# Thirteen loads of the next attention head, issued by ScalarE instead of SyncE

## The reference, cut to what matters

```
Q, K, V = proj(q_w), proj(k_w), proj(v_w)          # per head: two halves of 32, values of 64
attn1 = softmax(Q1 @ K1.T * scale)
attn2 = softmax(Q2 @ K2.T * scale)
out = (attn1 - lam * attn2) @ V                     # then an RMS norm over the head, an output projection
```

## Time and profile before

| | us |
|---|---|
| median of 3 runs | 6037.92 (6028.88 to 6040.64) |
| profiled execution | 6063.87 |
| its span on the core | 6062.1 |
| first and last `take_out` of the stage | 311.6 and 3228.1 |

### The profile page before, as it was taken

The page is one execution under the profiler, slowest core; times in us unless marked ns, Lnnn a source line. Parts: engine busy times, 40 slices in busy tenths (PEclk is TensorE's granted clock), DMA queues, the critical chain, the costliest instruction groups (busy, mean ns, idle before and its releaser), DMA issues. The chain is left out here.

```text
span 6062.1 us, 84099 instructions
## 1 busy us (share of the span) xinstructions
PE 5460.9 (90%) x23692; PEld 3112.7 (51%) x23692; DVE 3506.3 (58%) x4330; ACT 2393.7 (39%) x5287; POOL 3071.3 (51%) x1607
## 2 busy tenths in 40 slices
PE   8799999999999999999996979999997988897970
PEld 4455555555555555555553434554554555554540
DVE  3477777777777777777774543443443444443228
ACT  3255555555555555555552211322322333332430
POOL 0198888988888988888883102544441000000001
PEclk9799999999999999999997886999998999998995
DMA  6601111101111011111013643112201000000121
GB/s 224 190 16 40 41 42 42 37 19 42 42 42 42 18 39 40 42 41 41 15 41 94 179 147 73 37 37 53 58 16 61 21 21 21 21 10 30 47 92 69
DMA packets 244613, 330.97 MB, mean 55 GB/s; under 512 B 87260, under 2 KB 224754, under 8 KB 234490
## 3 DMA queue, kind: packets, MB, share of 16 engines
q1 hardware_dynamic: 244218, 326.08, 19.4%
HBM read 202.49 MB, written 123.51 MB: 54 GB/s over the span
## 5 line engine op out<-in xcount | busy, mean ns | idle before, releaser
L654 POOL TENSOR_TENSOR diff_run_pool<-diff_run_pool,diff_probs 128x768 f32<-128x768 f32 x1152 | 2235.1, 1940 | 187.8 <-ACT diff_probs L502 100.6
L582 DVE TENSOR_REDUCE diff_maxes<-diff_max 128x1 f32<-128x768 f32 x1752 | 1571.7, 950 | 676.3 <-PE diff_max L404 675.5
L502 ACT ACTIVATE diff_probs<-diff_ring 128x384 f32<-128x384 f32 x3462 | 1398.8, 495 | 956.9 <-PE diff_ring L394 843.0
L430 PE MATMUL diff_out_ps<-diff_probs,diff_vs 128*64 128x384 f32 x6912 | 1272.5, 504 | 0.0
L394 PE MATMUL diff_ring<-diff_qs,diff_ks 97*128 97x384 f32 x3462 | 1076.5, 385 | 19.6 <-issue 10.1
L404 PE MATMUL diff_max<-diff_ks,diff_qs 96*128 96x384 f32 x3504 | 953.9, 354 | 98.8 <-DVE diff_maxes L582 65.0
L394 PEld LDWEIGHTS diff_ring<-diff_qs,diff_ks 97*128 97x128 f32 x3462 | 607.3, 188 | 552.1 <-issue 360.1
L430 PEld LDWEIGHTS diff_out_ps<-diff_probs,diff_vs 128*64 128x64 f32 x6912 | 453.0, 139 | 559.3 <-issue 360.5
L404 PEld LDWEIGHTS diff_max<-diff_ks,diff_qs 96*128 96x128 f32 x3504 | 613.0, 193 | 148.3 <-DVE diff_maxes L582 95.5
L2083 POOL MEMSET pick_before<- 128x128 f32 x1 | 0.2, 204 | 1311.0 <-POOLq L63 1311.0
L1299 DVE TENSOR_REDUCE causal_maxes<-causal_max 128x1 f32<-128x384 f32 x522 | 288.7, 554 | 522.2 <-PE causal_max L1180 316.4
(11 more groups left out here) (228 smaller groups left out, 5935.9 us busy)
## 6 DMA issues: line engine op xcount, KB each, us to landing
diff_qs<-qk_hi SPq DMA_DIRECT2D x68, 288.0 KB, 7.7
diff_ks<-qk_hi SPq DMA_DIRECT2D x68, 288.0 KB, 10.1
diff_recip<-row_factors SPq DMA_DIRECT2D x194, 96.0 KB, 2.7
o_rows<-diff_normed SPq DMA_DIRECT2D x97, 192.0 KB, 1.8
qk_hi<-proj_hi SPq DMA_DIRECT2D x12, 1536.0 KB, 5.8
qk_lo<-proj_lo SPq DMA_DIRECT2D x12, 1536.0 KB, 9.6
causal_qa<-qk_hi SPq DMA_DIRECT2D x120, 96.0 KB, 2.5
diff_qs<-qk_lo SPq DMA_DIRECT2D x34, 288.0 KB, 8.8
```

Source lines behind the costliest of these rows:

```text
L430: mm = pe.matmul(out_ps[VD * j:VD * (j + 1), 0:T], vs[par][:, g, j, :], probs[g % PBUF][:, j * T:(j + 1) * T], start=g == 0, stop=g == STE ...
L502: act.activation(probs[g % PBUF][:, j * T:(j + 1) * T], ring[bank][:, 0:T], ACT.Exp, scale=SCALE).then_inc(s_taken, 1)
L582: dve.tensor_reduce(maxes[side][:, row:row + 1, h], max_ps[u % 2][:, :, 0:T], AX.XY, ALU.max).then_inc(s_red, 1)
L654: pool.tensor_tensor(run_pool[:], acc[:], probs[g % PBUF][:], ALU.add).then_inc(s_accp, 1)
```

## The change

ACT issues the 13 loads instead of SP. It does so in slot 0 of a head's first chunk, behind the six exponentials that it handles in that slot. SP no longer waits for the last product of values, and keeps the sums' trip and the stores. Since the loads' addresses are written out as constants, ACT's loop over 8 pairs of heads becomes straight code; PE, DVE and POOL keep their loops. The first head's loads stay on SP. In the kernel before, the second head's loads are issued ahead of chunk 0's work, behind the first head's; in the changed kernel they fall into chunk 0.

```diff
+        def load(eng, par, b, h):
+            for j in range(2):
+                for dst, kind, parts in ((qs, 0, (qh, qh, ql)), (ks, 1, (qh, ql, qh))):
+                    for r, src in enumerate(parts):
+                        eng.dma_start(dst[par][j][r * HD:(r + 1) * HD, :].bitcast(F32),
+                                      src[b * 2 * H0 + kind * H0 + h, j, :, :]).then_inc(s_ld[par], 16)
+            eng.dma_start(vs[par][:, :, 0, :], v_tiles[:, b * NT:(b + 1) * NT, h, :]).then_inc(s_ld[par], 16)
...
-                load(0)
+                load(sp, 0, 0, 0)
...
                 for q in range(CHUNKS):
-                    if q % NC == 0:
-
-                        sp.wait_ge(s_pv, q * BATCHES + BATCH)
-                        load(q // NC + 1)
                     invert_sums(q - 1)
                     store(q - 1)
...
-                with act.Fori(0, HEADS // 2) as i:
+                for i in range(HEADS // 2):
                     for m in range(2 * NC):
                         q, m1 = i * (2 * NC) + m, (m + 1) % (2 * NC)
                         for slot in range(BATCHES):
...
                                 exps(q + 1, 0)
+                            if slot == 0 and m % NC == 0:
+                                nxt = (q // NC + 1) % HEADS
+                                load(act, nxt % 2, nxt // H0, nxt % H0)
                             if slot == ROWS_AT:
```

More of the change, by code:

```diff
@@ L322, in differential_attention @@
             "normed_ready", "stored"))
+        qh = qk_hi.rearrange("b (h j d) n -> (b h) j d n", j=2, d=HD)
+        ql = qk_lo.rearrange("b (h j d) n -> (b h) j d n", j=2, d=HD)
+        v_tiles = v_rows.rearrange("(t p) (h d) -> p t h d", p=P, d=VD)
+        def load(eng, par, b, h):
[5 more added lines that the diff above has]
+            eng.dma_start(vs[par][:, :, 0, :], v_tiles[:, b * NT:(b + 1) * NT, h, :]).then_inc(s_ld[par], 16)
         with nc.Block() as block:
@@ L329, in _ @@
                 sp.dma_start(ident_sb[:], ident).then_inc(s_const, 16)
[L331 to L343, removed]
                 def invert_sums(q):
```

## The result

The changed kernel took 6162.67 us (median of 4 runs, 6136.54 to 6171.92) beside 6039.28 (4 runs) for the kernel before: a ratio of 1.0197, interval 1.0157 to 1.0236. Run again later (experiment 5), the ratio was 1.0107, 1.0076 to 1.0138, with a median of 6137.49 against 6064.34 for the kernel before. It is slower, as forecast, by 1 to 2%. The two intervals belong to one and the same pair of kernels and do not overlap, so a ratio here is good to about 1%, and smaller effects are read from the traces. Both medians lie above the range given (5998 to 6120).

What follows compares the result with a forecast made beforehand. PE is busy 90% of the span; row sums waiting behind loads at head starts were taken to cost 121.6 us. Terms 20 + 31.5 + 11.1 gave +62.6 on the median 6037.9: 6100 us, range 5998 to 6120.

Steps and rivals of the forecast that it cites:

- the sum over the first chunks: Attention stage, first chunks of heads: 20 us inside the body, 31.5 behind the branch, 11.1 in chunk 0, together +62.6 us.
- the first term: Eight head starts inside the loop's body: each 2.5 us slower than now, 20 us in all.
- the second: Seven head starts behind the branch: each 4.5 us slower than now, 31.5 us in all.
- the third: Chunk 0: 5.6 us for ACT's part and 5.5 for the wait that is left, 11.1 us.
- Part one: ACT's 13 issues take 6.1 us; exponentials come 3.6 us late, clock adds 2: a first chunk's first half 5.6 late.
- the price of the clock: PE's granted clock falls behind its stop for ACT's issues: put at 2 us per head start.
- Part two: Loads begin later: 2.5 us inside the body, 4.5 behind the branch, where only 1.1 of ACT's issue time is exposed.
- part four: ACT's loop as straight code: saves ACT's branch, 0.7 us at seven places; idle time hides the rest, costed at nothing.
- Part three: SP free of loads: row sums still held in SP's issue until loads are nearly through; compact sums at 483.4, not 480.90.
- the first rival: At head starts, SP's row sums pass ACT's loads: -23 us, about 6014; chance 0.33.
- its sign, a short issue: SP's issue of the row sums taking well under 5 us, or half a us, would show the sums passing the loads.
- The range: Whole kernel's time: 5998 to 6120 us, leaving out the cases near 5925 and 6180.

Runs made afterwards that it cites:

- experiment 5: The changed kernel run once more with more rounds, against the kernel before: ratio 1.0107, median 6137.49 us against 6064.34.
- experiment 3: The changed kernel with all 13 loads issued by ACT in slot 3 instead of slot 0, behind the row sums' trip: 6101.4 us, ratio 1.0058.
- experiment 1: The kernel before with only ACT's loop written out as straight code, loads still on SP: ratio 1.0049 to the kernel before.
- experiment 2: The changed kernel with 12 of ACT's loads in slot 0 and the values' load in slot 3: 6085.7 us, ratio 1.0023.
- experiment 6: The kernel before with straight code on ACT, loads on SP, and the wait for PE's bank given first: ratio 1.0023.
- experiment 8: The changed kernel with ACT's issues spread, two per slot from slot 3, and the wait for PE's bank given first: ratio 0.9835.

## Why the prediction was right or wrong

**Right: the side, and the sum over the first chunks.** From the starts of `take_out`: the eight first chunks inside the body grew from 37.99 to 40.27 in the mean, 18.2 us in all (forecast 20); the seven behind the branch from 36.98 to 42.30, 37.2 us (31.5); chunk 0 ended 7.4 us later (11.1). Together 62.8, against 62.6. That the two sums meet so closely is luck: the first term was 1.8 too high, the second 5.7 too low, the third 3.7 too high (the 480.8 in its working stands in no row).

**Part one** held: 13 issues in 6.1 us, a stop of PE of 3.3 us, the clock behind it. Only the price of the clock was low: experiment 3 has 6.6 us for such a stop alone, where I took 5.6. In the second head of the changed kernel the row sums are issued 16.9 us behind `take_out` instead of 10.5, 6.4 later; over the eight heads inside the body it is 15.6 in the mean, 5.1 later, where I had 5.6.

**Part two** held inside the body: the first load is issued 2.2 us behind `take_out` (2.5). Behind the branch it was issued 4.0 us behind it, but my claim that ACT's stop would be mostly covered there failed. With ACT's own branch gone, the clock did not fall in slot 0 (1.00 from 655 to 666 us, where it was 0.52 from 647 to 654 before), so PE ran into the full stop:

```profile
656.31 0.62 PE L388 MATMUL diff_ring<-diff_qs,diff_ks 97*128 97x384 f32 x2 [1.62 <-issue]
...
658.80 0.32 ACTq L332 DMA_DIRECT2D diff_qs<-qk_hi  x1
...
665.56 0.44 PE L388 MATMUL diff_ring<-diff_qs,diff_ks 97*128 97x384 f32 x1 [3.42 <-ACT diff_probs L496]
```

That is a stop of 3.42 us where I had 1.1. It lies ahead of the wait for the row sums, which becomes shorter by it, and is not what made the branch term 5.7 us short. By experiment 1 the shortfall belongs to part four: with straight code alone these chunks go from 36.98 to 38.28, 9.1 us over the seven, and with the loads on ACT from there to 42.30, 4.0 each, under my 4.5.

**Part three**, the heart, was right in what it costs and wrong in its place. The row sums are not held in SP's issue; they wait behind it, until the loads' packets are through. I had written that an issue of half a microsecond would mean that the first rival holds. It did not: the issue took 0.49 us and the landing 5.5. The rival in which the sums pass the loads is excluded, by the landing and by experiment 2; its sign, a short issue, came all the same, so the sign was badly chosen. By the Trainium skill, DMA: Bandwidth & Descriptors, "Queues, rings and completion order", each DMA engine takes turns between two rings packet by packet; these runs show no such turn, since the 3 KB waited for 4.7 us in the changed kernel (issued at 483.98, packets at 488.64) and ran only with the last packets of the loads. The same section of the Trainium skill says that neither SP nor ACT has a descriptor generator of its own. The order seen agrees with that; the hold in SP's issue that I had drawn from it did not come. Whether the order arises in the generation of descriptors or in the DMA engines stays open.

**Part four** is the step that failed. I costed straight code at nothing but a gain of 0.7 us at seven places. Experiment 1 has it at 21.9 us. In the changed kernel the chunks behind the first grew by 16 us (ordinary 29.45 to 29.50, last chunks 29.31 to 30.09), for which the sum had no term, and the chunks behind the branch grew more than forecast. I had looked at ACT's idle time in a slot, 2.2 us, and concluded that it hides everything. It hides instructions that run before PE's bank is full, and not quite one that stands between that event and the exponential: ACT is 0.08 us later in each slot, of which an ordinary chunk of six slots shows less than 0.1 in all. The order of the waits is worth 9.1 of the 21.9 us (experiment 6). Another 10 are the last chunks, which go with the slow scaling on DVE; it is slow in 2 and 5 heads of the two kernels with ACT's loop, and in 6 to 15 of those with straight code, and what straight code has to do with it stays open.

**The range** failed for a second reason, and this one carried the median out of it. 79 us of the 108 between the traces lie in the stage, and 6037.9 + 78.8 = 6117 would still have been inside. The remaining 29 are the causal stage, 984.5 against 954.5 us, which came back at 958.2, at a higher granted clock, in the repetition. The first medians lie 123 us apart, 15 more than the traces, and no row shows where. I had carried everything outside the stage over at no change and no spread. I took 0.2% for what a measurement can tell, and the medians of the kernel before alone moved from 6039 to 6064. A range from one stage's sum should have been widened by that.

**The cause of the excess before** is shown: with the loads behind the trip it is gone inside the body, whoever issues them. What cured it was when the loads start. Moving the issue to another engine cured nothing.

## What to carry to other kernels

A small DMA that the critical path waits for must be ahead of bulk loads in time; here another issuing engine did not take it past them. Before moving issues to a compute engine, set their time (here 0.47 us each) against that engine's idle time in one slot, and spread them if they do not fit. When a hardware loop is written out, look at which instruction carries the wait for the event that comes last.

## What the runs showed of the hardware that I had not expected

- A DMA of 3 KB from SP was accepted in 0.49 us while 13 loads issued by ACT were in flight, and held 7.2 to 7.6 us in the issue behind 13 of SP's own. Behind ACT's it took 5.5 to 7.4 us until it could be read back (first chunks inside the body); with only 12 loads of 9216-byte rows ahead, 4.9 to 5.4 us; with none, mostly 1.6 us.
- In straight code on ACT the exponential started 0.56 us behind PE's score, and 0.48 us with the bank's wait given first.
- A value scaling on DVE of one shape took 0.82 us in most places of one kernel and up to 2.50 us in others; the chunks in which it was slow took 0.8 us longer (29.2 and 30.0 us in the kernel before).
- With the loads out of the way and ACT's branch gone, the granted clock was 1.00 from 285 to 2700 us (experiment 8), although PE stood still for up to 1.7 us behind its own branch.
